# Beginning the walk on the input and deciding the first layer's experts late

## The reference

```
x = x + 0.5 * ffn(layernorm(x))    # mixture of 8 experts, top 2
x = x + attention(layernorm(x))    # 16 heads of 16, causal, over 1024 tokens of a batch
x = x + 0.5 * ffn(layernorm(x))
```

## Time and profile before

| what | value |
|---|---|
| device time, median of three runs | 1511.21 us |
| device time of the profiled execution | 1511.56 us |
| its span (first to last instruction) | 1509.8 us |
| TensorE busy | 1301.3 us (86%) |
| VectorE busy | 1122.5 us (74%) |
| ScalarE busy | 975.7 us (65%) |
| GpSimd busy | 412.8 us (27%) |
| mean granted TensorE clock (1 is full speed) | 0.956 |
| first projection of the walk begins | 93.83 us |

### The profile page before, as it was taken

How to read it: one execution, slowest core, us unless ns; L and a number is a source line. 1 busy time by engine, 2 the same in 40 slices (tenths; PEclk the granted TensorE clock), 3 DMA queues, 4 the chain that set the end, 5 groups by cost and what they waited for, 6 DMA issues and landing times.

```text
span 1509.8 us, 25323 instructions
## 1 busy us (share of the span) xinstructions
PE 1301.3 (86%) x8464; PEld 569.6 (38%) x8464; DVE 1122.5 (74%) x3677; ACT 975.7 (65%) x1729; POOL 412.8 (27%) x536
## 2 busy tenths in 40 slices
PE   2644789999999999899999999999999998999884
PEld 2421233334433443344434443344334443334332
DVE  6833788877788778877888778877877788868642
ACT  5411377767777677767777767667766776766761
POOL 2311223222322232323322232223322322222220
PEclk9877799999999999999999999999999999999996
DMA  8012412222322123222322232202322232221000
GB/s 254 1 32 59 117 46 67 71 53 60 87 60 68 37 58 81 64 64 64 81 63 64 52 85 62 66 28 63 92 64 53 63 87 60 67 54 43 1 1 29
DMA packets 53903, 95.07 MB, mean 63 GB/s; under 512 B 5776, under 2 KB 47376, under 8 KB 47632
## 3 DMA queue, kind: packets, MB, share of 16 engines
q1 hardware_dynamic: 51744, 92.29, 24.8%
q10 hardware_dynamic: 2032, 1.19, 0.3%
HBM read 59.91 MB, written 33.55 MB: 62 GB/s over the span
## 4 chain that ended last, share of the span: by engine, by line
PE 58%; ACT 15%; DVE 14%; issue 5%; POOL 3%; DMA 2%; DVEq 2%; SPq 0%; POOLq 0%; ACTq 0%
PE o_bank L1162 14%; PE s L1143 12%; PE st L1130 11%; PE misc L1088 7%; ACT q_stack L790 5%; DVE s L950 4%; ACT probs L803 4%; PE misc L1109 4%; PE misc L1083 3%; PE misc L501 3%; DVE max_full L954 2%; ACT parts L766 2%; ACT qk L766 2%; DMA part_dram<-parts 1%; DVE o_tok L1001 1%
## 5 line engine op out<-in xcount | busy, mean ns | idle before, releaser
L803 ACT ACTIVATE probs<-st 128x512 f32<-128x512 f32 (+1 forms) x1216 | 631.5, 581 | 203.0 <-PE st L1130 117.3
L950 DVE CUSTOM_DVE_ANT_0 s<-s,causal 128x128 f32<-128x128 f32 (+3 forms) x1024 | 493.8, 502 | 184.1 <-PE s L1143 179.9
L1143 PE MATMUL s<-k_stack,q_stack 96*128 96x512 bf16 (+3 forms) x1536 | 496.6, 335 | 54.9 <-DVE max_diag L950 23.8
L1130 PE MATMUL st<-q_stack,k_stack 108*128 108x512 bf16 (+3 forms) x1536 | 490.5, 332 | 21.0 <-ACT probs L803 18.6
L954 DVE TENSOR_REDUCE max_full<-s 128x1 f32<-128x512 f32 x512 | 349.9, 683 | 39.8 <-PE s L1143 38.3
L1162 PE MATMUL o_bank<-probs,v_aug 128*17 128x512 f32 (+3 forms) x3072 | 325.6, 496 | 19.3 <-ACT parts L766 9.2
L655 POOL TENSOR_SCALAR_AFFINE_SELECT probs<-probs 128x512 f32<-128x512 f32 x256 | 163.5, 640 | 537.9 <-ACT probs L803 537.7
L1143 PEld LDWEIGHTS s<-k_stack,q_stack 96*128 96x128 bf16 x1536 | 149.5, 98 | 413.2 <-DVE max_diag L950 179.8
L1130 PEld LDWEIGHTS st<-q_stack,k_stack 108*128 108x128 bf16 x1536 | 150.1, 99 | 142.6 <-ACT probs L803 63.8
L666 POOL TENSOR_TENSOR rest<-qk,parts 128x512 f32<-128x512 f32 x64 | 74.1, 1158 | 350.3 <-ACT parts L766 341.0
L790 ACT ACTIVATE q_stack<-misc 12x2048 bf16<-12x2048 f32 x64 | 119.7, 1870 | 74.5 <-PE misc L1115 73.1
(11 more groups left out here) (107 smaller groups left out, 920.3 us busy)
## 6 DMA issues: line engine op xcount, KB each, us to landing
part_dram<-parts SPq DMA_DIRECT2D x128, 192.0 KB, 2.8
q_stack<-part_dram SPq DMA_DIRECT2D x32, 384.0 KB
k_stack<-part_dram SPq DMA_DIRECT2D x32, 384.0 KB
x_all<-x SPq DMA_DIRECT2D x16, 512.0 KB, 5.7
q_stack<-part_dram SPq DMA_DIRECT2D x32, 256.0 KB
k_stack<-part_dram SPq DMA_DIRECT2D x32, 256.0 KB
out<-x_all SPq DMA_DIRECT2D x8, 1024.0 KB, 17.5
q_stack<-part_dram SPq DMA_DIRECT2D x32, 128.0 KB
```

The source lines that it names most:

```text
L803: nc.scalar.activation(probs[:, g % 2, h - part:h + 1, 0:width], st_bank[i % 3][:, 0:share * width] .rearrange("p (h c) -> p h c", c=width ...
L950: nc.vector.tensor_tensor_reduce(out=bank, in0=bank, in1=causal[:, CW - width:CW], scale=1.0, scalar=-BIG, op0=ALU.add, op1=ALU.max, accum ...
L1130: score = nc.tensor.matmul(st_bank[i % 3][:, part * width:(part + 1) * width], k_stack[0:KROWS + MROWS, hg, h, jb * P:(jb + 1) * P], q_sta ...
L1143: nc.tensor.matmul(s_bank[u % 3][:, 0:width], q_stack[0:KROWS, hm, h, ib * P:(ib + 1) * P], k_stack[0:KROWS, hm, h, j0:j0 + width], start= ...
```

## The change

The walk now begins on the input itself, as if the first layer added nothing. Its prologue (`prologue_plan(spec)`) holds the statistics, normalising and transposing of batch 0's two chunks, interleaved with the first projections. SyncE loads only the first four chunks of x at the start; the chunks of batch b + 2 are loaded at hg 1 of batch b ("xload"). ScalarE writes the constant rows of `k_stack` in the prologue, behind the v uses ("ones"). The weights' DMAs are issued in another order.

The first layer's logits are made inside the walk from the `x_t` that the attention uses anyway: uses `lg0` and `lt0`, two pairs at the end of the prologue and one pair in each of hg 2 and hg 3, at units 7 and 12, of batches 0 to 6. The twelve top-2 operations are spread over hg 1 of the last batch, at units 2, 6, ... 46; the counting stands at unit 2 and the decision at unit 10 of hg 2.

After the walk each engine loads the first flag. If it is set, x is loaded again, the experts of layer 0 run, and the whole walk runs a second time (`run`, `redo`), with a second set of semaphores (`Walk`). If not, each engine jumps over all of that. The last gate follows as before. `rest` is gone: GpSimd subtracts in `qk32` in place, and ScalarE waits for the third part before it writes `qk32` again. The two layers have their own `logits` and their own column of `flag`.

The diff, cut to its core (renamed semaphores are left out):

```diff
+TOP2_OPS = 12
-    "end": (24, 26, 29, 32, 35), "top2": 17,
+    "end": (24, 26, 29, 32, 35), "top2": 17, "before": (7, 12), "xload": 0, "top0": (2, 4), "count0": 2,
+    "decide0": 10,
...
+    if hg >= 2 and nxt and spec:
+        put(PLACE["before"][0], ("use", "lg0", hg - 2))
+        put(PLACE["before"][1], ("use", "lt0", hg - 2))
+    if hg == 1 and spec:
+        put(PLACE["xload"], ("xload",))
+    if not nxt and spec:
+        if hg == 1:
+            for k in range(TOP2_OPS):
+                put(PLACE["top0"][0] + PLACE["top0"][1] * k, ("top0", k))
+        if hg == 2:
+            put(PLACE["count0"], ("count0",))
+            put(PLACE["decide0"], ("decide0",))
...
-    plan = project(0, 0) + project(0, 1) + [(3, "use", "v", j) for j in range(4)]
+    plan = norm(0) + turn(0) + norm(1) + [(3, "weights",)] + project(0, 0) + turn(1) + project(0, 1)
+    plan += [(3, "use", "v", j) for j in range(4)] + [(3, "ones", hq) for hq in range(NG)]
+    if spec:
+        plan += [(3, "use", what, c) for c in range(2) for what in ("lg0", "lt0")]
...
+        def if_kept(eng, layer, body):
+            eng.wait_ge(flag_ready, layer + 1)
+            kept_here = eng.value_load(flag[0:1, layer:layer + 1], min_val=0, max_val=1)
+            with eng.If(kept_here > 0):
+                body()
+            with eng.Else():
+                eng.nop()
...
+        def run(eng, attention, moe, idle, ready):
+            attention(first)
+            idle()
+            def redo():
+                ready()
+                moe(0)
+                attention(again)
+            if_kept(eng, 0, redo)
...
+                elif kind == "xload":
+                    if b + 2 < B:
+                        for c in range(2):
+                            chunk = 2 * (b + 2) + c
+                            load_x(chunk, x_in[chunk % LOADS])
...
-                    wait(eng, rest_ready, lin(b, 2 * NG, 2 * m + c))
+                    wait(eng, sig.part3_ready, lin(b, 2 * NG, 2 * m + c))
...
-                    nc.gpsimd.tensor_tensor(rest[:, :], qk32[:, :], parts[:, c, 0, :], ALU.subtract)\
+                    nc.gpsimd.tensor_tensor(qk32[:, :], qk32[:, :], parts[:, c, 0, :], ALU.subtract)\
...
+                elif kind == "ones":
+                    if sig.spec:
+                        hq = a[0]
+                        eng.wait_ge(max_rows_ready, MPARTS)
+                        rows = nc.scalar.activation(k_stack[KROWS:P, hq, :, :],
+                                                    row_of_head[:, :, :].to_broadcast([32, HG, S]), ACT.Copy)
...
-            eng.wait_ge(gate_lt_taken, NCH)
-            top2(0, 0, NT)
-            count_and_decide(0)
-            moe_vector(0)
-            walk(handle)
-            eng.wait_ge(misc_free, COUNTS_AFTER["use"] + 1)
+            def idle():
+                eng.drain().then_inc(engine_idle, 1)
...
+            run(eng, attention, moe_vector, idle, ready)
             top2(1, TOP2_EARLY, NT)
-            count_and_decide(1)
-            moe_vector(1)
+            count_chosen(tables[1][0])
+            decide(1)
+            if_kept(eng, 1, lambda: moe_vector(1))
...
+                elif what == "lg0":
+                    last = tensor_gate_logits(misc, x_t[:, :, a[0] * CW:(a[0] + 1) * CW])
```

More of the change, by code:

```diff
@@ L263, in make_sections, with walk @@
     return out, before
-SECTIONS, COUNTS_AFTER = make_sections()
-def walk(handle):
-    for plan, times, b0, start in SECTIONS:
+PLANS = [make_sections(spec) for spec in (False, True)]
+def walk(sig, handle):
+    for plan, times, b0, start in PLANS[sig.spec][0]:
         for i in range(times):
@@ L337, in program @@
         lg_t = sb("lg_t", [P, P])
-        logits = sb("logits", [P, NT, E])
+        logits = [sb(f"logits{layer}", [P, NT, E]) for layer in range(2)]
         rank = sb("rank", [P, 1, E])
@@ L516, in moe_value, with moe_experts @@
             return c * TURNS + (e * EXPERT_TURNS + (GATE_TURNS + CHUNK_TURNS + turn))
-        def moe_experts(eng, layer, gate, chunk, expert):
+        def if_kept(eng, layer, body):
             eng.wait_ge(flag_ready, layer + 1)
-            kept_here = eng.value_load(flag[0:1, 0:1], min_val=0, max_val=1)
+            kept_here = eng.value_load(flag[0:1, layer:layer + 1], min_val=0, max_val=1)
             with eng.If(kept_here > 0):
[L523 to L536, removed]
+                body()
             with eng.Else():
                 eng.nop()
+        def moe_experts(eng, layer, gate, chunk, expert):
+            if gate:
+                gate()
+            with eng.Fori(0, NCH) as c:
+                if chunk:
+                    chunk(c, lambda turn: moe_value(c, None, turn))
+                with eng.Fori(0, E) as e:
+                    expert(c, e)
+            eng.wait_ge(baton[layer], GATE_TURNS + NCH * TURNS)
+        def run(eng, attention, moe, idle, ready):
[6 more added lines that the diff above has]
+            if_kept(eng, 0, redo)
         block = ctx.enter_context(nc.Block())
@@ L544, in _, with load_x @@
         def _(eng):
+            def load_x(chunk, landed):
+                eng.dma_start(x_tiles(chunk * CT, CT), x[chunk * CT:(chunk + 1) * CT, :, :].rearrange("t p d -> p t d"))\
+                   .then_inc(landed, 16)
             for k in range(LOADS):
[L546 to L554, removed]
+                load_x(k, x_in[k])
             def moe_sync(layer):
@@ L719, in _ @@
[L719 to L724 removed]
+            eng.dma_start(w_gate[:, :, 0:E], gate_t.rearrange("(c p) e -> p c e", p=P)).then_inc(gate_weight_in, 16)
             def moe_scalar(layer):
@@ L879, in count_and_decide, with count_chosen, decide @@
+            def top2(layer, t0, t1):
+                for k in range(TOP2_OPS):
+                    top2_op(logits[layer], tables[layer], t0, t1, k)
+            def count_chosen(chosen):
+                eng.drain()
+                nc.vector.tensor_reduce(counts[:, :], chosen.rearrange("p t e -> p e t"), AX.X, ALU.add)\
+                    .then_inc(counted, 1)
+            def decide(layer):
+                vec = nc.vector
                 eng.wait_ge(totalled, layer + 1)
@@ L977, in handle @@
                         if t == 0:
+                            if sig.spec and what == "next":
+                                chunk = 2 * (b + 1) + c
+                                eng.wait_ge(x_in[chunk % LOADS], 16 * (chunk // LOADS + 1))
                             eng.drain()
```

469 lines of the change are left out of this document (204 added, 265 removed).

## The result

The changed kernel takes 1463.9 us in the median of four runs (1462.96 to 1467.06), against 1512.93 of the kernel before in the runs beside it: ratio 0.9683, 95% interval 0.9664 to 0.9701, faster by 3.2%. The profiled execution took 1462.96 us with a span of 1461.2, 48.6 us less than the span before. The forecast was 1472, the range 1455 to 1491: direction and range hold, but that is in part luck: the term of the walk is off by 17.7 us, and errors of the other sign in the other terms cover 8 of them.

The account below looks back on a forecast made before the run. The prediction took the walk as bound by TensorE (92% busy), behind a serial start. Its terms, -64.9 + 18 + 6 + 2 = -38.9 us from 1511.56, less 0.35, gave about 1472 us, range 1455 to 1491.

Parts of the forecast that it names:

- Term 1: Start: beginning the walk on chunk 0 brings the first s matmul from 130.38 to 65.5 us, -64.9 us.
- Rival C: Start: GpSimd's 11.89 us gap shrinks with fewer x loads, up to 9.3 us earlier, total 1463 us; chance 0.12.
- Term 2: Walk: 14 lg0/lt0 pairs in hg 2 and 3 cost TensorE 1.3 us each, +18 us.
- Rival A: Walk: it absorbs the new lg0/lt0 uses, which cost 3 us instead of 18, total 1457 us; chance 0.20.
- The check by the earlier trace: Walk: step hg 2 to hg 3 took 2.91 us more with a gate, suggesting little of the added cost returns.
- Rival B: Walk: nothing is returned and lt0 waits too, so pairs cost 39 us, total 1493 us; chance 0.12.
- Term 3: Last batch: top-2 operations add 4 us in hg 1, counting and deciding 2 in hg 2, +6 us; GpSimd's reduction hidden.
- Term 4: Tail, before the last top-2: VectorE drains, loads a flag and jumps over experts and second walk, +2 us.
- Rival D: End of the walk: jumps over the second walk cost over 41 us in series, making the kernel slower; chance 0.03.
- Rival E: After the walk: flag 0 comes out set, the second walk runs and the time nearly doubles; chance 0.01.

Follow-up runs that it names:

- ones_later: Changed kernel with the four writes of k_stack's constant rows moved to units 10, 20, 30 and 40 of the prologue's score units: 1460.02 us.
- late_sum: Changed kernel with GpSimd's sum over partitions and the decision moved from hg 2 of the last batch to the epilogue, counts staying: 1458.51 us.
- short_jump: Changed kernel with the second walk left out of the jumped-over body, so the jump's target is near: 1460.92 us.
- no_pairs: Changed kernel without the 14 lg0/lt0 pairs in hg 2 and 3, first flag always written as 0: 1463.06 us.
- pairs_late: Changed kernel with the lg0/lt0 pairs at units 45 and 47 instead of 7 and 12: 1461.15 us.

## Why the prediction was right, and which terms were off

- *Term 1, the start, -64.9: right.* The path was the one named, uses of `misc` in series, then ScalarE's rows, then lg0 and lt0; the first s matmul came at 66.10 instead of 65.5. That the stack transfers are late next was right too (ones_later: 61.23, waiting for them). Some 2 us are lost behind it: the part from the first st to the first o_raw took 15.8 at a clock of 0.74 instead of 14.1 at 0.87. It is not the change that costs this: late_sum and short_jump, with the same prologue, take 14.4 and 14.2 there at 0.83 and 0.84.
- *Rival C, GpSimd's gap shrinks with fewer loads: wrong.* It lasts 12.43 with 2 MB of loads as it did 11.89 with 8.
- *Term 2, the walk, +18: the step that failed.* It measured +0.3. I named lg0's wait (0.95, measured 0.93) and the work (0.97) rightly and returned 0.6 of them; in truth 1.4 of 1.9 come back, 1.2 of it as the two waits for VectorE that are gone. I had returned only a part of one of them, on the ground that TensorE is the bound of the stretch; in units 4 to 20 VectorE was the fuller engine. And I gave TensorE's clock no part at all in the walk, since the mean of it was 0.98. That mean hid six short stretches at 0.79 to 0.89; with the pairs they are gone. Rival A was nearer with term 2 (3) and had half of the mechanism; its 1457 for the whole is 7 too low, since the other terms were too small. The check by the earlier trace rows, 2.91 for a step with a gate, was misleading: 0.4 of it was lost clock, and batch 1's step also has VectorE's statistics and normalising for the last gate. Rival B's sum was wrong by itself: 0.97 + 0.95 + 1.09 is 3.0 a pair and not 2.8, which makes 42 and not 39.
- *Term 3, the last batch, +6: too small by 3.3.* hg 1 grew by 2.8 where I took 4. hg 2 grew by 6.5 where I took 2. The step that failed is "GpSimd's reduction ... is hidden": I read its 0.43 us and not the idle time ahead of it. In the kernel before, both reductions stand behind waits for VectorE of 15.63 and 12.60, so no row could show it.
- *Term 4, the tail, +2: too small by 2.* The bounds from 1.42 to 11.89 held; the measured 4.3 is 1.7 for the near jump and 2.6 for the distance. The row of 1.42 was a near jump and priced only that.
- *Rival D, slower by jumps:* its mechanism is real and its price a tenth of what it needed. *Rival E:* the second walk was not entered.

## What to carry to other kernels

Before an added instruction is priced on the busiest engine, look at the stretch in which it will stand, with its granted clock: a piece of work that fills a wait costs only a part of itself (0.49 of 1.9 us here), and where the clock stays up with it, it can pay for that too, while the same piece a second time cost 1.26. A cost can hide in the idle time of an engine that is not on the path (GpSimd's 6 us in front of a reduction); it shows only when the instruction is moved to where that engine is needed. And a branch over much code belongs where its engine waits anyway.

## What the runs showed of the hardware

- TensorE's granted clock fell inside a walk that keeps it 92% busy: after waits of 0.49 and 0.72 us on VectorE, in stretches of 14 us, to a mean of 0.79 to 0.89, at a price of 0.3 to 1.9 us each. Where 17 more TensorE instructions stood in the same stretch it stayed at 1.00 in all six batches, though waits of 0.93 and 0.78 us were left in it.
- Which of these stretches lose clock differs between kernels that have the same work in them (hg 2 of batch 1: 15.65 in no_pairs, 14.57 in the kernel before). The five executions of pairs_late ran from 1460.3 to 1469.53, the slowest with the lowest mean clock (0.949 against 0.957 to 0.960).
- GpSimd stood idle 5.8 to 5.9 us in front of a reduction over partitions between other GpSimd work, and 7.1 us behind it and two masks.
- A jump over the experts alone put 0.53 us of "issue" on VectorE's path, one over a whole walk as well 3.14.
